# Edge network of a four-layer GNN kernel: sums by source node from three bf16 parts with bf16 one-hots, in place of f32 activations with f32 one-hots

## What is computed

```python
edge_in = jnp.concatenate([h[row], h[col], dist], axis=1)
e = jax.nn.silu(edge_in @ eW1 + eb1)
e = jax.nn.silu(e @ eW2 + eb2)
agg = jax.ops.segment_sum(e, row, num_segments=h.shape[0])
node_in = jnp.concatenate([h, agg], axis=1)
out = jax.nn.silu(node_in @ nW1 + nb1) @ nW2 + nb2
```

## Time and profile before

| | |
|---|---|
| median of 3 runs | 1738.2 us |
| the profiled execution | 1737.73 us |
| its span | 1735.7 us |
| mean granted TensorE clock | 0.932 |
| PE busy | 1461.2 us (84%) |
| DVE busy | 1141.1 us (66%) |
| ACT busy | 481.9 us (28%) |
| loop of the edge network, from its first layer-1 product to its last sum | 568.0 to 1017.9 us |

### The profile page before, as it was taken

The page is one execution under the profiler, slowest core; times in us unless marked ns, Lnnn a source line. Parts: engine busy times, 40 slices in busy tenths (PEclk is TensorE's granted clock), DMA queues, the critical chain, the costliest instruction groups (busy, mean ns, idle before and its releaser), DMA issues. The chain is left out here.

```text
span 1735.7 us, 43832 instructions
## 1 busy us (share of the span) xinstructions
PE 1461.2 (84%) x16295; PEld 1351.0 (78%) x16295; DVE 1141.1 (66%) x3435; ACT 481.9 (28%) x910; POOL 44.6 (3%) x64
## 2 busy tenths in 40 slices
PE   0845428996997999999999969689999999999993
PEld 0534316776997788888888858679999999999993
DVE  5999837884436455555555547667767677676775
ACT  0269718993102343443434321000000000000000
POOL 1100000000000000000000012000000000000000
PEclk9978759997999999999999989889999999999996
DMA  1000014442001644445232233000000000000000
GB/s 20 7 0 0 0 28 139 133 144 75 2 2 39 167 116 133 130 115 149 70 104 69 69 83 82 6 1 2 2 3 2 3 2 2 3 2 3 2 2 21
DMA packets 36999, 83.92 MB, mean 48 GB/s; under 512 B 22926, under 2 KB 23942, under 8 KB 36848
## 3 DMA queue, kind: packets, MB, share of 16 engines
q1 hardware_dynamic: 32216, 74.42, 15.1%
q10 hardware_dynamic: 4410, 7.43, 1.7%
q0 software_dynamic: 224, 0.13, 0.0%
HBM read 60.76 MB, written 21.14 MB: 47 GB/s over the span
## 5 line engine op out<-in xcount | busy, mean ns | idle before, releaser
L1705 PE MATMUL L_psA<-L_parts,mat 125*128 125x192 bf16 x6250 | 517.2, 246 | 0.0
L1705 PEld LDWEIGHTS L_psA<-L_parts,mat 125*128 125x128 bf16 x6250 | 515.5, 98 | 1.1 <-DVE L_parts L1783 1.0
L1174 PEld LDWEIGHTS L_ps_pre<-L_drow,mat 128*128 128x128 bf16 x2250 | 128.5, 98 | 30.3 <-issue 1.1
L1340 DVE TENSOR_TENSOR L_e<-L_ps_z,L_eb 128x512 f32<-128x512 f32 x76 | 52.5, 691 | 132.7 <-PE L_ps_z L1184 132.5
L1770 DVE TENSOR_REDUCE L_sumr<-L_psA 125x64 f32<-125x192 f32 x250 | 89.4, 358 | 76.4 <-PE L_psA L1705 74.2
L1174 PE MATMUL L_ps_pre<-L_drow,mat 128*128 128x32 bf16 (+3 forms) x2250 | 132.8, 212 | 0.0
L659 DVE TENSOR_TENSOR onehot<-iota_bf,codes 128x1024 bf16<-128x1024 bf16 x150 | 98.7, 686 | 29.8 <-PE ps_extra L722 23.0
L771 PE MATMUL L_psA<-L_gparts,mat 125*128 125x192 bf16 x1250 | 112.6, 253 | 4.5 <-DVE L_gparts L784 4.5
L1647 ACT COPY L_wk<-L_Wk 128x64 f32 (+1 forms) x10 | 2.0, 242 | 404.5 <-PE L_psA L1705 404.5
L771 PEld LDWEIGHTS L_psA<-L_gparts,mat 125*128 125x128 bf16 x1250 | 108.8, 102 | 5.5 <-DVE L_gparts L784 4.8
L1168 PE MATMUL L_ps_pre<-mat,L_pp 125*128 125x512 bf16 x375 | 102.9, 383 | 2.5 <-DVE L_pp L1306 2.5
(11 more groups left out here) (296 smaller groups left out, 2365.4 us busy)
## 6 DMA issues: line engine op xcount, KB each, us to landing
L_drow<-rows_d SPq DMA_DIRECT2D x25, 728.0 KB
m_d<-panel SPq DMA_DIRECT2D x25, 684.2 KB
mat<-rows_d SPq DMA_DIRECT2D x25, 640.0 KB, 4.3
mat<-m_d SPq DMA_DIRECT2D x16, 684.2 KB
mat<-m_d ACTq DMA_DIRECT2D x9, 684.2 KB
L_drow<-rows_d SPq DMA_DIRECT2D x25, 84.5 KB
m_d<-panel SPq DMA_DIRECT2D x25, 79.4 KB
mat<-m_d SPq DMA_DIRECT2D x16, 79.4 KB
```

The lines of the kernel that those rows point to most:

```text
L1174: last = nc.tensor.matmul(ps_pre[bank][:, to:to + n], w, drow[k][:, of:of + n], start=False, stop=(r == 2 and cc == pieces[-1][0]))
L1340: nc.vector.tensor_tensor(grp(e2_of(k, g)), grp(ps_z2[bank]), eb2[:].unsqueeze(1).broadcast_to([P, len(tiles), H]), ALU.add).then_inc(bias ...
L1705: last = nc.tensor.matmul(ps[:, 0:3 * D], t.mat[0:B, kb, b * B:b * B + P], parts[src][:, kb].rearrange("p r d -> p (r d)"), start=(kb == 0 ...
```

## The change

The f32 result of the second Silu is cut into three bf16 parts (high, middle, rest), which sum to it, and the products by source take the three parts one after the other with one-hots in bf16. ACT makes the high part with a Silu of its own and the f32 value with a second one; DVE subtracts the high part from the f32 value in place (`cut_high`), ACT copies what is left to bf16 (`mid_part`), and DVE subtracts that to get the third part (`cut_mid`). The source codes are stored four times side by side (`DUP` = 4) in bf16 for the comparison. `silu2` and the cuts of a group stand in pass g+2, ahead of silu1 on ACT and ahead of add_bias on DVE; add_bias stays in pass g+1, and by_src in pass g+3. `e2` has two buffers in place of four. The diff, cut:

```diff
-        codes = [sb(f"scodes{i}", [P, ST], F32) for i in range(2)]
-        hot = [sb(f"hot{i}", [P, 4, B], F32) for i in range(2)]
+        codes = [sb(f"scodes{i}", [P, ST, DUP], BF16) for i in range(2)]
+        hot = [sb(f"hot{i}", [P, 4, P], BF16) for i in range(2)]
...
+        e2 = [sb(f"e2_{i}", [P, 4 * H], F32) for i in range(2)]
+        e2_parts = [room[:, o + i * 12 * H:o + (i + 1) * 12 * H].rearrange("p (r n) -> p r n", r=3) for i in range(2)]
+        buf = lambda k, g: (k * len(EG) + g) % 2
...
                 def by_src(b, k, g):
-                    pe.wait_ge(silu2_done, done(b, g))
+                    pe.wait_ge(split_done, done(b, g))
...
-                        last = nc.tensor.matmul(ps_agg[k][:, 0:B], e2_of(k, g)[:, i * H:(i + 1) * H],
-                                                hot[bank][:, i, :], start=(cc == 0), stop=(cc == ST - 1))
+                        for part in range(3):
+                            last = nc.tensor.matmul(ps_agg[k][:, 0:B], e2_parts[bank][:, part, i * H:(i + 1) * H],
+                                                    hot[bank][:, i, 0:B], start=(cc == 0 and part == 0),
+                                                    stop=(cc == ST - 1 and part == 2))
...
                 def silu2(b, k, g):
-                    e = e2_of(k, g)[:, 0:len(EG[g]) * H]
+                    e = e2[buf(k, g)][:]
                     act.wait_ge(biased, done(b, g))
+                    if not (first(b) and g < 2):
+                        act.wait_ge(seg_done, done(b, g) - 2)
+                    nc.scalar.activation(e2_parts[buf(k, g)][:, 0, :], e, ACT.Silu)
                     nc.scalar.activation(e, e, ACT.Silu).then_inc(silu2_done, 1)
+
+                def mid_part(b, k, g):
+                    act.wait_ge(cut, done(b, g))
+                    nc.scalar.copy(e2_parts[buf(k, g)][:, 1, :], e2[buf(k, g)][:]).then_inc(mid_done, 1)
...
                     for g in range(NG):
                         if was and g == 3:
                             keep_agg(*was)
+                        for group in before(b, k, g, 2):
+                            silu2(*group)
+                            mid_part(*group)
                         silu1(b, k, g)
...
-                        for group in before(b, k, g, 1):
-                            silu2(*group)
...
                 def add_bias(b, k, g):
                     dve.wait_ge(z2_done, NG * b + g + 1)
-                    if not (first(b) and g < 3):
-                        dve.wait_ge(seg_done, done(b, g) - 3)
...
+                def cut_high(b, k, g):
+                    e = e2[buf(k, g)][:]
+                    dve.wait_ge(silu2_done, done(b, g))
+                    nc.vector.tensor_tensor(e, e, e2_parts[buf(k, g)][:, 0, :], ALU.subtract).then_inc(cut, 1)
+
+                def cut_mid(b, k, g):
+                    part = e2_parts[buf(k, g)]
+                    dve.wait_ge(mid_done, done(b, g))
+                    nc.vector.tensor_tensor(part[:, 2, :], e2[buf(k, g)][:], part[:, 1, :], ALU.subtract
+                                            ).then_inc(split_done, 1)
 
                 def src_one_hots(b, k, g):
                     bank, n = (k * NG + g) % 2, len(EG[g])
+                    by4 = [P, n, P // DUP, DUP]
...
-                        hot[bank][:, 0:n, :], c.iota1[:, 0:B].unsqueeze(1).broadcast_to([P, n, B]),
-                        codes[k][:, EG[g][0]:EG[g][0] + n].unsqueeze(2).broadcast_to([P, n, B]), ALU.is_equal
+                        hot[bank][:].rearrange("p e (m t) -> p e m t", t=DUP),
+                        c.iota1_bf[:].rearrange("p (m t) -> p m t", t=DUP).unsqueeze(1).broadcast_to(by4),
+                        codes[k][:, EG[g][0]:EG[g][0] + n, :].unsqueeze(2).broadcast_to(by4), ALU.is_equal
...
                         if g == 4:
                             split_p(b + 1, 1 - k)
+                        for group in before(b, k, g, 2):
+                            cut_high(*group)
+                            src_one_hots(*group)
+                            cut_mid(*group)
                         for group in before(b, k, g, 1):
                             add_bias(*group)
-                        for group in before(b, k, g, 2):
-                            src_one_hots(*group)
```

More of the change, by code:

```diff
@@ L1003, in edge_network @@
         pp = [sb(f"pp{i}", [B, 3, H], BF16) for i in range(2)]
-        codes = [sb(f"scodes{i}", [P, ST], F32) for i in range(2)]
-        hot = [sb(f"hot{i}", [P, 4, B], F32) for i in range(2)]
+        codes = [sb(f"scodes{i}", [P, ST, DUP], BF16) for i in range(2)]
+        hot = [sb(f"hot{i}", [P, 4, P], BF16) for i in range(2)]
         e1 = [sb("e1", [H, 4 * P], F32), rest2]
         o += 16 * H
-        e2 = [sb(f"e2_{i}", [P, 4 * H], F32)[:] for i in range(2)]
-        e2 += [room[:, o + i * 8 * H:o + (i + 1) * 8 * H].bitcast(F32) for i in range(2)]
-        o += 16 * H
+        e2 = [sb(f"e2_{i}", [P, 4 * H], F32) for i in range(2)]
+        e2_parts = [room[:, o + i * 12 * H:o + (i + 1) * 12 * H].rearrange("p (r n) -> p r n", r=3) for i in range(2)]
+        o += 24 * H
         assert o <= (NB - HEAD) * MW
-        e2_of = lambda k, g: e2[(0, 1, 2, 0, 1, 2, 0, 1, 2, 3)[k * len(EG) + g]]
+        buf = lambda k, g: (k * len(EG) + g) % 2
         aggs = [sb(f"aggs{i}", [H, B], F32) for i in range(2)]
@@ L1114, in edge_network @@
         (panels_in, rows_hot, staged, pre_done, e1_ready, z2_done, biased, silu2_done,
-         hot_ready, seg_done, agg_ready, n1_ready, z1_ready, out_ready, out_kept, stats, xs_ready, p_ps, p_ready, var,
+         cut, mid_done, split_done, hot_ready, seg_done, agg_ready, n1_ready, z1_ready, out_ready, out_kept, stats, xs_ready, p_ps, p_ready, var,
          root, step) = map(sem, (
              "panels_in", "rows_hot", "codes_staged", "pre_done", "e1_ready", "z2_done", "biased", "silu2_done",
-             "onehots_ready", "seg_done", "agg_ready", "n1_ready", "z1_ready", "out_ready", "out_kept", "stats_taken",
+             "high_cut", "mid_done", "split_done", "onehots_ready", "seg_done", "agg_ready", "n1_ready", "z1_ready", "out_ready", "out_kept", "stats_taken",
              "xs_ready", "p_product", "p_ready", "var_ready", "std_ready", "net_step"))
@@ L1283, in _ @@
                 z = NB - 1
-                silu2(z, 0, NG - 1)
+                for g in (NG - 2, NG - 1):
+                    silu2(z, 0, g)
+                    mid_part(z, 0, g)
                 keep_agg(z, 0)
@@ L1323, in rows_to_hot @@
                         dve.wait_ge(hot_ready, NG * (b - 1) + 1)
-                    nc.vector.tensor_copy(codes[k][:], t.dense[:, bass.ds(b, 1), :].rearrange("p o t -> p (o t)")
-                                          ).then_inc(staged, 1)
+                    nc.vector.tensor_copy(
+                        codes[k][:], t.dense[:, bass.ds(b, 1), :].rearrange("p o t -> p (o t)").unsqueeze(2)
+                        .broadcast_to([P, ST, DUP])).then_inc(staged, 1)
                     dve.wait_ge(src_in[k], 8 * (b - k) + 16)
@@ L1336, in add_bias @@
                     dve.wait_ge(z2_done, NG * b + g + 1)
-                    if not (first(b) and g < 3):
-                        dve.wait_ge(seg_done, done(b, g) - 3)
[L1339 to L1342, removed]
+                    nc.vector.tensor_tensor(
+                        e2[buf(k, g)][:].rearrange("p (i h) -> p i h", h=H),
+                        ps_z2[bank][:].rearrange("p (i h) -> p i h", h=H),
+                        eb2[:].unsqueeze(1).broadcast_to([P, len(tiles), H]), ALU.add).then_inc(biased, 1)
+                def cut_high(b, k, g):
[7 more added lines that the diff above has]
+                                            ).then_inc(split_done, 1)
                 def src_one_hots(b, k, g):
                     bank, n = (k * NG + g) % 2, len(EG[g])
+                    by4 = [P, n, P // DUP, DUP]
                     if not (first(b) and g < 2):
@@ L1377, in _ @@
                 z = NB - 1
-                add_bias(z, 0, NG - 1)
-                src_one_hots(z, 0, NG - 2)
-                src_one_hots(z, 0, NG - 1)
+                for g in (NG - 2, NG - 1):
+                    cut_high(z, 0, g)
+                    src_one_hots(z, 0, g)
+                    cut_mid(z, 0, g)
+                    if g == NG - 2:
+                        add_bias(z, 0, NG - 1)
                 keep_out(NB - 1, 0)
```

## The result

The changed kernel takes 1809.6 us, the median of 4 runs (1804.7 to 1814.3), against 1738.0 before. The ratio is 1.0411, with a 95% interval of 1.0383 to 1.0440: clearly slower, within the range of 1780 to 1838, and 10.6 us above the 1799 predicted. The profiled execution took 1809.05 us with a span of 1805.9 and a mean granted clock of 0.922.

What follows compares the result with a forecast made beforehand. The hand-off of one group between DVE and ACT, not PE, would bound the loop: 124 rings (479.9 us), late starts (19.7) and the last group end it 60.9 us later, 1737.7 + 60.9 = 1798.6 us; range 1780 to 1838.

Steps and rivals of the forecast that it cites:

- What bounds the kernel: PE bounds the loop before; after the change the order of DVE's and ACT's steps does, giving 1799 us.
- two views that looked like spare time: Rival for the loop: PE stays the bound and its saving shows, 26 us less, 1712 us; chance 0.04.
- PE's gain: Products by source: 12 bf16 products in 0.68 us replace 0.89 us per group; PE saves 1.05 us per block.
- The ring: From add_bias through both Silus, cut_high, mid_part and cut_mid to the next add_bias on DVE and ACT: 3.87 us per group.
- The cover of the one-hot: One-hot between cut_high and cut_mid on DVE: up to about 0.76 us is hidden, so its gain is worth nothing.
- Once per block: On DVE, dst_rows_to_hot and split_p make cut_high start 0.82 us late, 24 times: 19.7 us.
- PE under the ring: PE has 16.85 us of work per 20.2 us block; its tightest place is product_p in pass 3, waiting for stage_x.
- slack of 1.1 us: At product_p in pass 3: PE's work behind it would finish 1.1 us before add_bias(3) wants it.
- rival of the low clock: PE, idle 3.3 us per block, drops to its lower clock: 34 us in a tenth of the blocks, 1832; chance 0.03.
- The sum: Whole loop: 479.9 us for 124 rings, 19.7 for late starts, then the last group; last keep_agg 60.9 us later, 1798.6.

Runs made afterwards that it cites:

- run with both edits: Changed kernel with add_bias between the cuts on DVE, and node_silu and stage_x of pass 3 between silu2 and mid_part on ACT: 1720.4 us.
- run with spare one-hots: Changed kernel with each one-hot instruction of DVE issued a second time, into a buffer that nothing reads: 1807.5 us.

## Why the prediction was right, and what it missed

- **What bounds the kernel.** Right. The two views that looked like spare time (idle DVE and ACT, by sums still under PE's block) would have given 1712. Reading who stands behind whom gave 1799.
- **PE's gain.** 12 sums take 0.72 us (855.01 to 855.73 from weight load to weight load) where I had 0.68. The run with both edits had blocks of 16.85 and 16.98 us, 16.91 on average, against 16.85. In the changed kernel it is worth nothing.
- **The ring.** Its six terms were 0.72, 0.53, 0.66, 0.71, 0.65, 0.60; measured 0.72, 0.54, 0.65, 0.72, 0.65, 0.61. The sum was 3.87, measured 3.88 to 3.89. The estimate of 3.69 from the table in the Trainium skill (VectorE: DVE Perf Modes, section "The TRN2 errata") is 0.2 short here. The same section says that the table's VectorE row is too low for a single instruction and gives 691 ns for an f32 addition of two tensors of 512 elements. The trace agrees: the cuts, which are subtractions with one bf16 operand, take 0.69 us each.
- **The cover of the one-hot.** Right: 0.42 us, and a second one beside it cost nothing.
- **Once per block.** The pass is 4.68 us (848.55 to 853.23), 0.79 longer, against 0.82. A block at full clock is 20.29 or 20.37 us, in turn, against 20.17; 0.06 to 0.08 of the difference is the pass with `keep_out`.
- **PE under the ring.** This is the step that was mis-sized. I gave `product_p` a slack of 1.1 us and held the low clock to be a rival of 0.03 chance. The slack was right at full clock: layer2(3) is over at 852.08 (850.97 + 1.11), and its `add_bias` starts at 853.23. So `product_p` alone does not hold the ring. But PE waits 1.9 us there in 23 of 23 blocks, the clock falls after it in 7 of them, and then layer2(3) is late by up to 0.5 us. The rival of the low clock thus happened, at 3.7 us in these blocks in place of the 34 that I gave it.
- **The sum.** From first to last `add_bias` I had 499.6 us, measured 508.9. By the starts of `add_bias` the 9.3 come from three terms. The ring is 3.885 and not 3.87, 124 times: 1.9 us. The pass with `keep_out` and every second one after it are 0.08 longer, for which I had nothing: 2.9 us. The long passes are 24.3 us over the ring in place of 19.7: 4.6 us, of which 3.7 are the 7 blocks at the lower clock and 1.3 the last block's pass, also at the lower clock, for which I had nothing. The last group's sums ran at the low clock too (granted 0.50 from 1085 to 1088 us): 5.5 us from the last `add_bias` to `keep_agg`, 0.7 above my 4.8. The earlier start takes 0.8 off. Together 9.2, which is 70.1 against 60.9. The rest up to the median of 1809.6 lies outside the span: the profiled execution took 3.2 us more than its span, where it had been 2.0, and it lies 0.5 below the median.

The low clock in one block and not in another shows in layer 1's 15 products behind `product_p` and in the `add_bias` that waits for what follows them:

```profile
603.45 1.73 PE L1173 MATMUL L_ps_pre<-L_drow,mat 128*128 128x96 bf16 x15
...
607.01 0.69 DVE L1350 TENSOR_TENSOR L_e<-L_ps_z,L_eb 128x512 f32<-128x512 f32 x1 [0.45 <-PE L_ps_z L1183]
...
849.96 0.96 PE L1173 MATMUL L_ps_pre<-L_drow,mat 128*128 128x96 bf16 x15
...
853.23 0.68 DVE L1350 TENSOR_TENSOR L_e<-L_ps_z,L_eb 128x512 f32<-128x512 f32 x1
```

It also shows in two pairs of windows, each PE's wait for `product_p` and what follows it:

```profile
599.80:602.20 2.40, 0.54 (x10) 0.36 (x7) 2.04 (x4) 1.65 (x4) 0.00 (x0) 1.00 0.03 7
602.20:605.40 3.20, 3.16 (x23) 2.61 (x23) 3.10 (x8) 1.33 (x3) 0.00 (x0) 0.62 0.00 0
...
867.30:869.30 2.00, 0.10 (x3) 0.03 (x1) 1.65 (x4) 1.65 (x4) 0.00 (x0) 1.00 0.00 0
869.30:872.00 2.70, 2.70 (x29) 2.33 (x30) 2.60 (x7) 1.15 (x2) 0.00 (x0) 1.00 0.00 0
```

The first wait is followed by a granted clock of 0.62 on average, that is mostly 1.2 GHz, the second by 1.00. The two waits are alike. There is a pattern in it: the blocks with the slow products are 0, 1, 2, 4 and from there every fourth, up to 24, and the run with spare one-hots has the same ones. What decides between them no run here tells, nor whether it is why the runs of the changed kernel spread more widely than those with `stage_x` early.

## What to carry to other kernels

Idle time on an engine is an offer only for work that no one waits for in turn. Before adding a step to a software pipeline, write down for each engine what stands behind it in program order, and follow one group round until you are back at the same step: the ring's time, not the busy share, then sets the least time of a block. Where it is too long, a change in one engine's order can be worth more than the arithmetic saved: here 76 us for `add_bias` between the cuts, against the 17 us by which the best order tried is faster than the kernel before. And where two late paths lead into the same instruction, taking away one can show little: here 0.1 and 4.5 us each, and 22.7 both.

## What was not expected of the hardware

PE's clock fell after waits of about 2 us in a loop where PE was busy for 87% of the time, and in some blocks only: the mean from 600 to 980 us was 0.97, 0.95 with `dst_rows_to_hot` in pass 1, 0.94 with `add_bias` first, where the wait was 2.4 us, and 1.00 in every run in which PE did not wait at `product_p` or waited 0.7 us at most. The earlier stage of the earlier trace rows that had kept 1.00 at 8.17 us busy in 10 was no guide to this loop.
